# Layer 0 of a one-core language-model tower: items prepared one turn nearer to their use, GpSimd's work in item order

## The reference, cut to what matters

```python
h = take(W.T, x)                                  # (16, 256) ids -> (16, 256, 256) float32
x = _layernorm(h)                                 # no scale or shift
for l in range(6):
    residual = x
    n = _layernorm(x, gamma[l], beta[l])
    q, k, v = split(n @ w_qkv[l], 3)
    q = softmax(q, axis=1);  k = softmax(k, axis=2)
    context = einsum('bic,bjc->bij', k, v)
    out = einsum('bic,bij->bjc', q, context) @ w_out[l] + b_out[l]
    x = out + residual
h = h + x
h = h + ffn(_layernorm(h))                        # 8 experts, two chosen per token, and a shared one
```

## Time and profile before

| | us |
|---|---|
| median of 3 runs | 1397.06 (1396.82 to 1399.38) |
| profiled execution, device time | 1408.61 |
| its span | 1406.8 |
| TensorE busy, share of the span | 1265.1, 90% |
| VectorE | 1026.0, 73% |
| ScalarE | 871.0, 62% |
| GpSimd | 847.4, 60% |
| mean granted TensorE clock | 0.959 of full speed |

### The profile page before, as it was taken

How to read it: one execution, slowest core, us unless ns; L and a number is a source line. 1 busy time by engine, 2 the same in 40 slices (tenths; PEclk the granted TensorE clock), 3 DMA queues, 4 the chain that set the end, 5 groups by cost and what they waited for, 6 DMA issues and landing times.

```text
span 1406.8 us, 36953 instructions
## 1 busy us (share of the span) xinstructions
PE 1265.1 (90%) x10994; PEld 1058.2 (75%) x10995; DVE 1026.0 (73%) x2647; ACT 871.0 (62%) x2377; POOL 847.4 (60%) x870
## 2 busy tenths in 40 slices
PE   3415889999999999999999999886999999999996
PEld 3414677888888888888888888753566888888885
DVE  2346899999999999999898899863565555554543
ACT  3204678899889988988988888744542332323331
POOL 3057787677677767767787877547552243434343
PEclk8757999999999999999999999998999999999998
DMA  9943655644544553225233755414434444444440
GB/s 338 372 132 90 143 135 137 175 112 128 134 106 114 134 137 80 65 60 138 67 67 73 171 101 97 76 34 133 115 113 138 74 62 67 64 69 64 66 62 13
DMA packets 349078, 156.66 MB, mean 111 GB/s; under 512 B 279856, under 2 KB 333392, under 8 KB 349008
## 3 DMA queue, kind: packets, MB, share of 16 engines
q1 hardware_dynamic: 315168, 116.92, 34.1%
q0 software_dynamic: 20112, 25.32, 10.3%
q10 hardware_dynamic: 13728, 13.63, 2.7%
HBM read 44.62 MB, written 43.16 MB: 62 GB/s over the span
## 4 chain that ended last, share of the span: by engine, by line
PE 70%; issue 7%; DVE 7%; ACT 6%; DMA 4%; POOL 3%; SPq 1%; ACTq 1%; another core or an unknown queue 0%; POOLq 0%; DVEq 0%
PE bank L852 33%; PE bank L953 14%; PE bank L969 7%; PE bank L900 5%; PE bank L984 5%; PE bank L1001 3%; PE bank L904 2%; DMA emb<-Wall 1%; ACT bank L1200 1%; ACT EQhl L1204 1%; DMA Wall<-in_L_tok_W 1%; DVE X L1421 1%; ACT PR L1209 1%; DMA Wall<-emb,Wall 1%; PE bank L832 1%
## 5 line engine op out<-in xcount | busy, mean ns | idle before, releaser
L852 PE MATMUL bank<-hT,Wc 128*128 128x256 f16 x2304 | 286.9, 275 | 43.3 <-DMA hT<-hhl 29.8
L852 PEld LDWEIGHTS bank<-hT,Wc 128*128 128x128 f16 x2304 | 227.2, 99 | 71.7 <-issue 43.8
L807 POOL DMA_INDIRECT out_rows<-h0b,payin x78 | 121.5, 1558 | 208.8 <-DVE h0b L1696 177.2
L953 PE MATMUL bank<-xTg,Wall 128*128 128x256 f16 x1872 | 211.0, 273 | 1.1 <-DMA xTg<-slot_x 1.1
L953 PEld LDWEIGHTS bank<-xTg,Wall 128*128 x1872 | 182.8, 98 | 23.2 <-issue 1.8
L688 POOL TENSOR_TENSOR h0b<-h0b,rows 128x512 f32<-128x512 f32 x80 | 101.3, 1267 | 138.2 <-DVE h0b L1411 88.1
L1229 ACT ACTIVATE silu<-bank 128x512 f32<-128x512 f32 x110 | 65.5, 595 | 188.9 <-PE bank L953 135.2
L1366 DVE SCALAR_TENSOR_TENSOR gT<-bank,silu 128x512 f32<-128x512 f32 x110 | 75.9, 691 | 116.5 <-ACT silu L1229 100.1
L852 PE MATMUL bank<-Wc,MT 128*128 128x256 f16 x1152 | 142.7, 274 | 12.6 <-DVE MT L1457 12.6
L852 PE MATMUL bank<-Wc,hT 128*128 128x256 f16 x1152 | 144.0, 276 | 0.1
L852 PE MATMUL bank<-khl,eqT 128*128 128x256 f16 x1152 | 141.3, 272 | 1.3 <-DVE khl L1469 0.2
(11 more groups left out here) (178 smaller groups left out, 2593.4 us busy)
## 6 DMA issues: line engine op xcount, KB each, us to landing
Wall<-in_L_tok_W SPq DMA_DIRECT2D x25, 512.0 KB, 8.5
emb<-Wall ACTq DMA_DIRECT2D x25, 512.0 KB, 9.6
Wall<-in_L_ffn_ew SPq DMA_DIRECT2D x24, 512.0 KB, 4.1
Wc<-Wn SPq DMA_DIRECT2D x40, 128.0 KB, 2.6
Wst<-in_L_attn_w_qkv SPq DMA_DIRECT2D x12, 384.0 KB
h_rows<-Wall SPq DMA_DIRECT2D x8, 512.0 KB
X<-h_rows POOLq DMA_DIRECT2D x8, 512.0 KB, 6.2
out_rows<-X SPq DMA_DIRECT2D x8, 512.0 KB
```

Source lines behind the costliest of these rows:

```text
L807: pool.indirect_dma_start(out=out_rows, out_offset=bass.IndirectOffsetOnAxis(ap=got(j % PAYS, w, 0, i32), axis=0), in_=yout[j % 2][:, w, : ...
L852: last = mm(to, lhs(a, k, o), moving, start=(i == 0 and k == 0), stop=(i == 2 and k == 1))
L953: last = mm(to, cols(a, e, 2 * k + w, (2 * half + c) * P, P), moving, start=(n_ == 0), stop=(n_ == 5))
```

## The change

In layer 0 alone (`early(u)`: items 0 to 15), VectorE does norm and first_x for item t+4 instead of t+5, and stats and mean for t+5 instead of t+7. first_x moves behind the mean at the end of the turn. ScalarE does hh for item t+3 instead of t+4 (or t+5), and SyncE transposes item t+3. GpSimd handles one item in a run: hf(t+4), roots(t+5), gather(t+7), low(t+4); before turn 0 the gather stands behind low. gamma writes into `hf` instead of back into `xn`. norm waits for the gamma of the item before (`s_hg`) instead of its beta (`s_hf`). Where layer 0 passes into layer 1 both distances stand in a turn: in turn 10 stats of items 15 and 16, in turn 11 norm of items 15 and 16 (16 at the very end of the turn), in turn 12 hh and `turn_h` of items 15 and 16. `HEAD` rises from 12 to 14, since these turns must be written out.

```diff
-        HEAD, FIRST_CUT = 12, 3
+        HEAD, FIRST_CUT = 14, 3
@@ SyncE
             def turns(t, p):
-                if have(t + 4):
-                    turn_h(t + 4 if isinstance(t, int) else sp.snap(t + 4), p)
+                if early(t + 3):
+                    turn_h(t + 3, 1 - p)
+                if have(t + 4) and not early(t + 4):
+                    turn_h(t + 4, p)
-            turns(-4, 0)
@@ GpSimd
-                if have(t + 4) and not (isinstance(t, int) and t < 0):
+                def roots_first():
+                    pool.wait_ge(s_amv, u + 1)
+                    ...
+                    pool.tensor_tensor(erstd[1 - p][:, :], evar[1 - p][:, :], mhalf[:, 0:2 * TB], ALU.pow).then_inc(s_arstd, 1)
+
+                if early(t + 4):
+                    pool.wait_ge(s_rows, 48)
+                    pool.wait_ge(s_xn, t + 5)
+                    if t > -4:
+                        pool.wait_ge(s_h, t + 4)
+                    pool.tensor_tensor(hf[:, :, :], xn[:, :, :], row(0, 0), ALU.mult).then_inc(s_hg, 1)
+                    pool.wait_ge(s_hg, t + 5)
+                    pool.tensor_tensor(hf[:, :, :], hf[:, :, :], row(1, 0), ALU.add).then_inc(s_hf, 1)
+                    if early(u):
+                        roots_first()
+                    if t >= 0 and early(t + 7):
+                        gather_item(t + 7)
+                    pool.wait_ge(s_hh, t + 5)
+                    low_half()
+                    if t < 0:
+                        gather_item(t + 7)
+                elif have(t + 4):
                     pool.wait_ge(s_hh, t + 5)
                     pool.sem_inc(s_passed, 1)
-                    low_half(t + 4, p)
+                    low_half()
+                elif t == -6:
+                    gather_item(1)
+                elif t == -5:
+                    roots_first()
+                    gather_item(2)
+                if have(u) and not early(u):
                     ... (gamma, bias and beta of item t+5, as before)
@@ ScalarE
-                i = t + 5 if isinstance(t, int) and t < -1 else t + 4
-                if have(i) and not (isinstance(t, int) and t == -1):
+                if early(t + 3):
+                    act.wait_ge(s_hf, t + 4)
+                    if t + 3 >= 2:
+                        act.wait_ge(s_hT[1 - p], landed(t + 1))
+                    A(hhl[1 - p][:, 0, :, :], hf[:, :, :], ACT.Copy).then_inc(s_hh, 1)
+                if have(t + 4) and not early(t + 4):
+                    act.wait_ge(s_hf, t + 5)
+                    ...
+                    A(hhl[p][:, 0, :, :], hf[:, :, :], ACT.Copy).then_inc(s_hh, 1)
@@ VectorE
             def norm(w, p):
                 dve.wait_ge(s_arstd, w + 1)
-                wait(dve, s_hf, w)
                 if early(w):
+                    wait(dve, s_hg, w)
+                    wait(dve, s_xb, w)
...
-                if have(t + 5):
+                if early(t + 4):
+                    norm(t + 4, p)
+                elif have(t + 5) and not early(t + 5):
                     norm(t + 5, 1 - p)
...
-                if early(t + 5):
-                    first_x(t + 5, 1 - p)
-                if early(t + 7):
-                    v = t + 7
+                if early(v):                      # v = t + 5
...
-                if early(t + 7) and have(u):
-                    first_mean(t + 7, 1 - p)
+                if have(u) and early(v) and early(v + 1):
+                    first_mean(v, 1 - p)
+                if early(t + 4):
+                    first_x(t + 4)
...
+                if early(t + 4) and not early(t + 5):
+                    dve.wait_ge(s_xb, t + 5)
+                    norm(t + 5, 1 - p)
```

More of the change, by code:

```diff
@@ L661, in one, with low_half @@
                 u, w = t + 5, t + 6
-                row = lambda r: rows[:, bass.ds(layer(u) % 2, 1), r, :].broadcast_to([P, TB, D])
-                def low_half(i, q):
-                    pool.tensor_tensor(hhl[q][:, 1, :, :], hf[:, :, :], hhl[q][:, 0, :, :], ALU.subtract).then_inc(s_h, 1)
-                if have(t + 4) and not (isinstance(t, int) and t < 0):
+                row = lambda r, l: rows[:, bass.ds(l % 2, 1), r, :].broadcast_to([P, TB, D])
+                def low_half():
+                    pool.tensor_tensor(hhl[p][:, 1, :, :], hf[:, :, :], hhl[p][:, 0, :, :], ALU.subtract).then_inc(s_h, 1)
@@ L687, in one @@
                     pool.sem_inc(s_passed, 1)
-                    pool.tensor_tensor(xn[:, :, :], xn[:, :, :], row(0), ALU.mult).then_inc(s_hg, 1)
-                    pool.tensor_tensor(tiles(u), tiles(u), row(2), ALU.add).then_inc(s_xb, 1)
+                    pool.tensor_tensor(xn[:, :, :], xn[:, :, :], row(0, layer(u)), ALU.mult).then_inc(s_hg, 1)
+                    pool.tensor_tensor(tiles(u), tiles(u), row(2, layer(u)), ALU.add).then_inc(s_xb, 1)
                     pool.wait_ge(s_hg, u + 1)
-                    wait(pool, s_h, u)
+                    pool.wait_ge(s_h, u)
                     pool.sem_inc(s_passed, 1)
-                    pool.tensor_tensor(hf[:, :, :], xn[:, :, :], row(1), ALU.add).then_inc(s_hf, 1)
-                elif t == -7:
-                    gather_item(1)
-                elif t == -6:
-                    gather_item(2)
-                w = t + 7 if early(t + 7) else t + 6
-                if early(w) and t == w - 7:
-                    pool.wait_ge(s_amv, w + 1)
-                    if w >= 2:
-                        pool.wait_ge(s_xb, w - 1)
-                    pool.tensor_scalar(evar[1 - p][:, TB:], amv[1 - p][:, :, 1], EPS, None, ALU.add)
-                    pool.tensor_scalar(evar[1 - p][:, 0:TB], amv[1 - p][:, :, 1], 1.0 + EPS, EPS * EPS, ALU.mult, ALU.add).then_inc(s_avar, 1)
-                    pool.wait_ge(s_avar, w + 1)
-                    pool.tensor_tensor(erstd[1 - p][:, :], evar[1 - p][:, :], mhalf[:, 0:2 * TB], ALU.pow).then_inc(s_arstd, 1)
-                elif have(w) and not early(w):
+                    pool.tensor_tensor(hf[:, :, :], xn[:, :, :], row(1, layer(u)), ALU.add).then_inc(s_hf, 1)
+                if have(w) and not early(w):
                     pool.wait_ge(s_amv, w + 1)
                     pool.tensor_tensor(avar[:, :], amv[p][:, :, 1], epst[:, :], ALU.add).then_inc(s_avar, 1)
-                if have(w) and not early(w):
                     pool.wait_ge(s_avar, w + 1)
@@ L1178, in one @@
                     last.then_inc(s_khi, 1)
-                i = t + 5 if isinstance(t, int) and t < -1 else t + 4
-                if have(i) and not (isinstance(t, int) and t == -1):
-                    q = i % 2 if isinstance(i, int) else p
-                    act.wait_ge(s_hf, i + 1)
-                    if not (isinstance(i, int) and i < 2):
-                        act.wait_ge(s_hT[q], landed(i - 2))
+                if early(t + 3):
[5 more added lines that the diff above has]
+                    act.wait_ge(s_hf, t + 5)
+                    act.wait_ge(s_hT[p], landed(t + 2))
                     act.sem_inc(s_passed, 1)
-                    A(hhl[q][:, 0, :, :], hf[:, :, :], ACT.Copy).then_inc(s_hh, 1)
+                    A(hhl[p][:, 0, :, :], hf[:, :, :], ACT.Copy).then_inc(s_hh, 1)
                 if c is not None:
@@ L1409, in norm @@
                     return
+                wait(dve, s_hf, w)
                 for k in range(TB):
@@ L1413, in norm, with first_x @@
                 last.then_inc(s_xn, 1)
-            def first_x(w, p):
+            def first_x(w):
                 dve.wait_ge(s_rows, 48)
@@ L1441, in one @@
             def one(t, p, kind, c):
-                u, w = t + 2, t + 6
+                u, v, w = t + 2, t + 5, t + 6
                 if have(u - 1):
@@ L1488, in one @@
                         V.bn_stats(stats[:, k, :], G[:, v * TB + k, :]).then_inc(s_astat, 1)
-                    if not have(u):
+                    if not have(u) or not early(v + 1):
                         first_mean(v, 1 - p)
@@ L1492, in one @@
                     dve.wait_ge(s_x, w + 1)
+                    if early(v):
+                        dve.wait_ge(s_amv, v + 1)
                     for k in range(TB):
```

19 lines of the change are left out of this document (5 added, 14 removed).

## The result

Both kernels were timed side by side on one chip, twelve executions each: 1398.16 us before and 1393.58 us after, the medians. By the medians the change gains 4.6 us. I had forecast 7.3 us of gain (1389.8 us) and a range of 1382 to 1398. So the direction was right and the time lies in the range, but the gain is well over a third smaller than forecast. Against the 1397.06 us from which my forecast started, the median of three executions, it is 3.5 us.

A forecast was written before the change was run, and what follows sets the result against it. Bounds: GpSimd at the start, nearly full VectorE and GpSimd in turns 1 to 9, then TensorE. m(10) 17.9 us earlier, partly paid back entering layer 1, left 7.3: 1397.06 - 7.3 = 1389.8 us, range 1382 to 1398.

The forecast's parts named there:

- The start: Before turn 1: with fewer items ahead, m(1) moves from 138.38 to 123.9 us, 14.5 us gained.
- TensorE's lower clock: First products at the start: up to 3 us more, not taken into the sum, kept for the range.
- The stall: Turn 2: VectorE's 3.7 us wait for gathered rows and the clock's fall behind it should go.
- the burst: Turn 2: the loads meet hT(4), which may land 2.3 us late; 2 us taken, 0 to 4 in the range.
- Turns 3 to 9: Seven turns at 9.1 us each, 63.7 us in all, bringing m(10) to 209.3 us.
- VectorE's loop: VectorE's work per turn: 9.5 us less what first_x may save, 8.1 us at best.
- GpSimd's loop: GpSimd's work per turn: 8.73 us with cut, about 9.1 to 9.3 with delays against first_x.
- an item's path: From low(i) through transpose, products and GpSimd to low(i+2): some 18 us for two turns, 9.0 to 9.5 a turn.
- The signs: For the middle turns: 9.1 to 9.3 us each, VectorE less full than before, GpSimd over 8.5 us.
- The handover: Passing into layer 1: TensorE idles 5.5 us, slow products add 2.5; m(14) only 7.3 us earlier; 4.5 to 9 in the range.
- ScalarE's wait: Turn 12: between hh(15) and hh(16), GpSimd's low(15), gamma, bias and beta of item 16 take 5.1 us.
- the slow products: Turn 12: TensorE's products behind its 5.5 us idle time run at lower clock, 2.5 us added.

The follow-up runs named there:

- a3: The changed kernel with GpSimd's order hf, roots, cut, low, gather, so the gather is last; ratio 0.9948, m(16) 183.1 us behind the first gather.
- a12: The changed kernel with VectorE's eratio right behind mlo, everything else kept; ratio 0.9980, m(16) 187.6 us behind the first gather.
- b2: The kernel before with the loads of layer 1's rows issued in turn 9 instead of turn 0; ratio 0.9971.
- a11: The changed kernel with gather last, hh(15) earlier, item 16's bias behind beta, first_x right behind norm, and layer 1's rows loaded in turn 9; ratio 1.0031.
- a1: The changed kernel with ScalarE's hh(16) behind the exponentials and PR in turn 12; ratio 0.9961, turn 12 12.65 us.
- a10: The changed kernel with GpSimd's gather last, hh(15) in ScalarE's turn 11, item 16's bias behind beta, and first_x right behind norm; ratio 1.0049.
- b1: The kernel before with ScalarE's hh(3) in turn -1 instead of turn -2; ratio 0.9959.
- c1: The kernel before with hh(3) in ScalarE's next turn and layer 1's rows loaded in turn 9; ratio 0.9925.

## Why the prediction was right in direction and too large

*The start: right.* The chain gamma, hh, low, transpose, then one GpSimd turn per item, gave every first product to 1.2 us, and m(1) to 1.7 us. Of this 1.7, 0.6 us is the first gather, which itself starts at 81.67 us instead of 81.07. TensorE's lower clock in q(0) and k(0) (2.72 and 2.76 us, granted 0.50), which I had kept for the range, came to nothing, as the path ran over GpSimd.

*Turns 1 and 2: pessimistic.* The stall went as forecast, since the gather is a turn further ahead. The 2 us that I added for hT(4) in the burst didn't reach m: q(4) waited 1.15 us, inside the turn. Turn 2 took 9.19 us and not 11.4.

*Turns 3 to 9: the step that failed.* I had put VectorE's loop at 8.1 us at best and set it aside, and had 9.1 us a turn from GpSimd's loop and an item's path. The signs that I named for this turned out the other way: VectorE is busy for all of turns 7 and 8, fuller than before and not less full, and GpSimd for 7.79 and 8.38 us, not for over 8.5. I had granted that first_x would meet gamma and beta. That it did: 1.43 us instead of 0.87. What I had not asked is who meets low and cut once first_x has left them. It was eratio, two operations of one column, at 1.71 us for 0.33. Both delays together are 1.94 us a turn; first_x's was 1.42 in before. VectorE was full and GpSimd waited for it. So seven turns took 67.9 us where I had 63.7: 4.2 us, the largest error of the sum, and 9.70 us a turn lies outside the 8.7 to 9.5 that I had allowed. a3 and a12 show that this delay was on the path, by taking the collision away or moving it.

The rule that I named (the Trainium skill, page "SBUF — State Buffer", section "SBUF: two separate sides": an exclusive lock for operations of VectorE with two SBUF inputs, held for the whole instruction) agrees with the rows in that eratio lasts as long as low and cut, and I had used it for first_x alone. Taken through all of VectorE's operations of a turn it would have named eratio as well. The same section says that whichever starts first keeps the ports and the other waits. The traces bear this out only in part. In b2 first_x keeps its 0.87 us and cut, which starts 0.5 us after it, takes 0.89 us instead of 0.66. In a11 first_x's first operation starts at 115.04 us, 0.38 us ahead of gamma, and takes 1.95 us instead of 0.47, while gamma takes 1.28 (1.27 alone).

*The handover: right in size, incomplete in cause.* ScalarE's wait was 5.1 us in the forecast and 5.04 measured. TensorE's gap was 5.5 and is 4.55, and the four turns took 41.1 us, not 42.4. Of the slow products that I had put at 2.5 us, a part came: o at 1.57 and 1.06 us for 1.03 and 0.60, and m(13) at 2.22 for 1.47, together some 1.7 (granted clock 0.66 from 242 to 247 us). But a second wait of 3.3 us lay beneath (norm(17) for arstd(17)), unseen in the forecast; a1 uncovered it.

*From the trace to the time.* Added up, +1.7 at the start, -2.8 in turns 1 and 2, +4.2 and -1.3 give 1.8 us less gain than forecast: 5.5 at m(14). The timed gain is 4.6. Counted from the first gather, the traced gain at m(14) is 6.1 us, and 1.5 us are missing. Up to m(14) they have no place in the trace. Behind it, the shared program doesn't repeat to this size: from m(14) to m(94) it took 651.1 us in before, 652.1 in after, 652.4 in the second trace of each, and 650.3 to 652.6 over all kernels. Nor is the gap special to this kernel. Against the mean of before's two traces, the gain by the medians was 0.4 to 4.5 us smaller than the traced one to m(16) in all kernels but a10 and a11 (b2: 8.0 to m(16), 4.4 by the medians). One reading is that before's stall, which differed by 1.6 us between its two traces, is shorter on average when no profile is taken. But b1 has that stall too, at 13.88 us, and its gap is still 2.1 us, so this can't be the whole of it. No run shows the cause, and it stays open. The ends of my range, added up from their terms (start, turns, burst, handover), come to 1380.3 and 1398.7, not to 1379 and 1400.

## What to carry to other kernels

When an operation is moved away from a collision between VectorE and GpSimd, ask which operation takes its place beside the same GpSimd work; a tiny one can be held as long as a large one, and what counts is what is queued behind it. Lay such operations beside DMA issues, and operations on PSUM beside GpSimd's tensor work: here the order of GpSimd's work alone was worth 4.5 us to m(16), where the whole change had 6.1. A long wait can cover another on the next engine, so price a chain by what stands behind its second longest wait too, and shorten the chain rather than pass it on.

## What was not expected of the hardware

- Two VectorE operations on 128x1 took 1.71 us beside GpSimd's low and cut, and 0.33 beside its gathers. The fp32 norm on one input, 128x256, took 1.64 us beside low and 0.72 else, while in a3 mlo, which reads PSUM, kept 0.86 us beside cut, as it has elsewhere.
- The delay falls mostly on VectorE, in a11 even where VectorE starts first: there first_x took 3.36 us beside gamma and beta, which took 1.28 and 1.34 themselves (1.27 alone), and its first operation had started 0.38 us before gamma. In b2 it fell on GpSimd: cut took 0.89 us instead of 0.66 behind first_x, which kept 0.87.
- Turns 5 to 8 hold the same operations in before, b2 and c1, and took about 9.5, 8.8 and 9.4 us, according to what lay beside first_x. What happened turns earlier decided it, and not the stall as such, since c1 has none.
- Three small loads of rows at the start of layer 0 made a 13.8 to 15.4 us turn out of one of 9.1, by delaying gathered rows.
